# Gated attention layer on one core: the channel mix drawn into the attention's program

## The reference

```python
    x = x + jnp.tanh(g_xattn[0]) * _L0_xattn_ref(_layernorm(x, axis=-1), ctx_1024, ctx_1024, mask_BxS2_if1, ...)
    x = x + jnp.tanh(g_ffn[0]) * _L0_ffn_ref(_layernorm(x, axis=-1), L0_ffn_W_r, L0_ffn_W_k, L0_ffn_W_v, L0_ffn_mu_r, L0_ffn_mu_k)
```

```python
            x_prev = jnp.concatenate([jnp.zeros((B, 1, C), x.dtype), x[:, :-1, :]], axis=1)
            xr = mu_r * x + (1.0 - mu_r) * x_prev
            xk = mu_k * x + (1.0 - mu_k) * x_prev
            r = jax.nn.sigmoid(jnp.einsum('btc,dc->btd', xr, W_r))
            k = jnp.einsum('btc,dc->btd', xk, W_k)
            k_act = jnp.square(jax.nn.relu(k))
            out = r * jnp.einsum('btc,dc->btd', k_act, W_v)
```

## Time and profile before

| | us |
|---|---|
| median of 3 runs | 2034.28 (2032.4 to 2034.94) |
| the profiled execution's own time | 2038.13 |
| its span, first to last instruction | 2036.4 |
| PE busy | 1932.5 (95%) |
| DVE busy | 1379.0 (68%) |
| POOL busy | 1295.2 (64%) |
| ACT busy | 971.1 (48%) |

### The profile page before, as it was taken

How to read it: one execution, slowest core, us unless ns; L and a number is a source line. 1 busy time by engine, 2 the same in 40 slices (tenths; PEclk the granted TensorE clock), 3 DMA queues, 4 the chain that set the end, 5 groups by cost and what they waited for, 6 DMA issues and landing times. The chain is left out here.

```text
span 2036.4 us, 36616 instructions
## 1 busy us (share of the span) xinstructions
PE 1932.5 (95%) x11648; PEld 1501.0 (74%) x11648; DVE 1379.0 (68%) x3534; ACT 971.1 (48%) x1870; POOL 1295.2 (64%) x1829
## 2 busy tenths in 40 slices
PE   5899999999999999999999999995599999999999
PEld 3677777777777777777777777772488888888887
DVE  3777777776777767777677777764466575656663
ACT  3555555555555555555555555544243433334341
POOL 4566666666666666666666666656277787777771
PEclk8999999999999999999999999996799999999999
DMA  5545555455554455545555445552122323132211
GB/s 182 108 114 123 128 144 124 113 123 126 144 123 114 122 128 144 118 119 121 129 144 118 118 123 127 126 145 64 62 83 82 103 72 113 67 106 74 98 67 62
DMA packets 128665, 229.31 MB, mean 113 GB/s; under 512 B 18656, under 2 KB 20704, under 8 KB 127616
## 3 DMA queue, kind: packets, MB, share of 16 engines
q1 hardware_dynamic: 128512, 227.43, 42.2%
HBM read 92.06 MB, written 33.59 MB: 62 GB/s over the span
## 5 line engine op out<-in xcount | busy, mean ns | idle before, releaser
L701 DVE CUSTOM_DVE_ANT_0 score_ps<-score_ps,causal 128x128 f32<-128x128 f32 (+3 forms) x1024 | 487.1, 504 | 295.1 <-PE score_ps L855 294.0
L533 ACT ACTIVATE probs<-prob_ps 128x512 f32<-128x512 f32 (+1 forms) x768 | 395.7, 527 | 412.3 <-PE prob_ps L879 209.2
L855 PE MATMUL score_ps<-k_stack,q_stack 97*128 97x128 f32 (+3 forms) x1024 | 319.5, 353 | 6.6 <-DVE least L701 2.9
L879 PE MATMUL prob_ps<-q_stack,k_stack 100*128 100x512 f32 (+3 forms) x1024 | 285.6, 320 | 20.4 <-DMA q_stack<-max_rows 14.3
L385 POOL TENSOR_SCALAR_AFFINE_SELECT probs<-probs 128x256 f32<-128x256 f32 x256 | 106.5, 416 | 271.7 <-ACT probs L533 271.7
L396 POOL TENSOR_TENSOR prob_sum<-probs 128x384 f32<-128x384 f32 x256 | 263.9, 1031 | 0.0
L855 PEld LDWEIGHTS score_ps<-k_stack,q_stack 97*128 97x128 f32 x1024 | 189.4, 191 | 53.5 <-issue 13.3
L879 PEld LDWEIGHTS prob_ps<-q_stack,k_stack 100*128 100x128 f32 x1024 | 193.6, 192 | 42.8 <-DMA q_stack<-max_rows 19.1
L399 POOL TENSOR_TENSOR prob_sum<-prob_sum,probs 128x256 f32<-128x256 f32 x256 | 188.8, 738 | 36.7
L389 POOL TENSOR_SCALAR_AFFINE_SELECT probs<-probs 128x256 f32<-128x256 f32 x256 | 105.0, 410 | 157.0 <-ACT probs L533 156.8
L896 PE MATMUL value_ps<-probs,v 128*32 128x512 f32 (+3 forms) x2048 | 154.8, 443 | 13.2 <-POOL prob_sum L399 13.2
(11 more groups left out here) (145 smaller groups left out, 4918.0 us busy)
## 6 DMA issues: line engine op xcount, KB each, us to landing
k_stack<-staged_k_high SPq DMA_DIRECT2D x256, 128.0 KB
q_stack<-staged_q_high SPq DMA_DIRECT2D x256, 128.0 KB, 3.1
tiles<-in_x SPq DMA_DIRECT2D x16, 1024.0 KB, 5.7
k_stack<-staged_k_low SPq DMA_DIRECT2D x128, 128.0 KB
q_stack<-staged_q_low SPq DMA_DIRECT2D x128, 128.0 KB, 3.2
x_io<-in_x SPq DMA_DIRECT2D x16, 1024.0 KB, 7.2
x<-x_io SPq DMA_DIRECT2D x64, 256.0 KB, 3.3
wk_low_room<-x SPq DMA_DIRECT2D x16, 1024.0 KB, 5.5
```

The lines of the kernel that those rows point to most:

```text
L533: nc.scalar.activation(probs[:, u % RING, lo:hi], prob_ps[(3 * u + c) % 2][:, 0:hi - lo], ACT.Exp, scale=SCALE).then_inc(exp_done, 1)
L701: nc.vector.tensor_tensor_reduce(out=here, in0=here, in1=causal[:, LATE - P * t:S], scale=-1.0, scalar=3e38, op0=ALU.add, op1=ALU.min, acc ...
L855: last = nc.tensor.matmul(here[:, at:at + P * (t + 1)], q_stack[n][0:MASK_ROW + 1, j, P * t:P * t + P], k_stack[n][0:MASK_ROW + 1, j, 0:P ...
L879: last = nc.tensor.matmul(here[:, at:at + width], k_stack[n][0:ROWS, j, P * k:P * k + P], q_stack[n][0:ROWS, j, P * k:S], start=True, stop ...
```

## The change

The two blocks become one function, `gated_layer`. Rooms are shared inside it: the mixed parts lie where Wq and Wk lay, squares where q and k were staged, gates, result and Wv in the stacks. The hardware loop is written out.

1. The tables. `WORK` is as before. A second table holds PE's pieces for slots N-4 to N+2, where fk and fr are the k and r projections of the channel mix of batch 0. The transposes of x1 of batch 0 stand in slots N-6 and N-5.

```diff
+        LAST_WORK = {
+            N - 4: ("", "", ""),
+            N - 3: ("", "fk0 0", "fk0 12"),
+            N - 2: ("fk0 3", "fk1 01", "fk1 23"),
+            N - 1: ("fk2 01", "fk2 23", "fk3 01"),
+            N: ("", "fk3 23", "fr0 01"),
+            N + 1: ("fr0 23", "fr1 01", "fr1 23"),
+            N + 2: ("fr2 0", "fr2 12", "fr2 3"),
+        }
```

```diff
+            def scale_earlier(e):
...
+                wait(act, mixed_done, e - 1)
+                col = "kr".index(n)
+                nc.scalar.activation(earlier[:, e % 2, 1:S], ffn_xT[:, k, 0:S - 1], ACT.Identity, scale=mu_rest[:, col, k:k + 1]
+                                     ).then_inc(scaled, 1)
...
+            def mix_tokens(e):
+                j, n, k = mix_tile(e)
+                dve.wait_ge(scaled, e + 1)
+                dve.wait_ge(mu_loaded, 16 * 2)
+                wait(dve, mix_low, e - 1)
```

3. The layernorm of the channel mix is applied by ACT instead of POOL. The relu goes straight into `square`, which DVE squares in place:

```diff
+                nc.scalar.activation(square[:, g, :], k_ps[g % 2][:], ACT.Relu).then_inc(relu_done, 1)
...
+                nc.vector.tensor_tensor(square[:, g, :], square[:, g, :], square[:, g, :], ALU.mult).then_inc(square_done, 1)
```

5. ACT's mixing work in the last slots (the tiles of batch 0 on DVE stand beside it in the same slots):

```diff
+                if i == N - 4:
+                    split_ffn("r")
+                    high_part_mix(1)
+                    scale_earlier(2)
+                if i == N - 3:
+                    scale_earlier(4)
+                    high_part_mix(3)
```

6. ACT in a round j of the rest, after its relus and casts:

```diff
-                gate_r(i, 0)
-                if has_next:
-                    high_part_mix(i + 1, "k", 0, k_done)
-                    high_part_mix(i + 1, "k", 1, k_done)
-                gate_r(i, 1)
...
+                for m in range(T):
+                    gate_r(j, m)
+                if j + 1 < B:
+                    mix_steps(j + 1, "k")
+                    mix_steps(j + 1, "r")
+                if j + 2 < B:
+                    for m in range(T):
+                        apply_layernorm(B + j + 2, m)
```

7. PE after the slots: the last r block, the last `values`, transposes of batch 1, the output projection of batch 15, and then the v projection of batch 0 and the rounds 1 to 15:

```diff
+            for k in range(K):
+                project_fr(0, 3, k)
+            values(N // HG - 1)
+            transpose_x(B + 1, 0)
+            transpose_x(B + 1, 1)
...
+            def project_fv(j, m, k):
...
+                elif k == 0:
+                    pe.wait_ge(y_done, T * j + m - 1)
```

More of the change, by code:

```diff
@@ L563, in first, with gate_r @@
+            def gate_r(j, m):
+                act.wait_ge(fr_done, T * j + m + 1)
+                act.wait_ge(y_done, T * (j - 1) + m + 1)
+                nc.scalar.activation(r_tanh[:, m, :], r_ps[m % 2][:], ACT.Tanh, scale=0.5).then_inc(r_ready, 1)
             def first(i, b, s):
@@ L612, in fourth @@
                     high_part_c(b + 1, 2 * (s - 11) + 1)
-                if has_next and b >= 0 and s in (6, 7):
+                if now and s in (6, 7):
                     apply_layernorm(b + 1, 2 * (s - 6) + 1)
@@ L780, in third @@
                     normalise((i - VALUES) // HG)
-                if has_next and b >= 0 and s == 3:
+                if now and s == 3:
                     layernorm_stats(b + 1, 0)
+                if i == N - 4:
+                    mix_tokens(1)
+                    low_part_mix(0)
+                if i == N - 3:
+                    low_part_mix(2)
+                if i == N - 2:
+                    mix_tokens(4)
+                    low_part_mix(4)
+                if i == N - 1:
+                    square_k(0, 1)
+                if i == N:
+                    for m in range(T):
+                        layernorm_stats(B + 1, m)
                 if has_next and s == 10:
@@ L840, in _, with mix_k, mix_r_and_combine @@
                 slot(i)
+            def mix_k(j):
+                e = 2 * K * j
+                mix_tokens(e)
+                for k in range(1, K):
+                    mix_tokens(e + k)
+                    low_part_mix(e + k - 1)
+                low_part_mix(e + K - 1)
+            def mix_r_and_combine(j):
+                e = 2 * K * (j + 1) + K
+                mix_tokens(e)
+                for k in range(1, K):
+                    mix_tokens(e + k)
+                    low_part_mix(e + k - 1)
+                    combine(j, k - 1)
+                low_part_mix(e + K - 1)
+                combine(j, K - 1)
+            correct(N // HG - 1)
+            refine(N // HG - 1)
+            normalise(N // HG - 1)
+            low_part_attn(N // HG - 1)
+            for m in range(T):
+                add_output(B - 1, m)
+            mix_k(1)
+            for m in range(T):
+                layernorm_stats(B + 2, m)
+            aggregate_stats(B + 2)
+            mix_r_and_combine(0)
+            for j in range(1, B):
+                for g in range(K):
+                    square_k(j, g)
+                if j + 2 < B:
+                    for m in range(T):
+                        layernorm_stats(B + j + 2, m)
+                    aggregate_stats(B + j + 2)
+                if j + 1 < B:
+                    mix_k(j + 1)
+                    mix_r_and_combine(j)
+                else:
+                    for m in range(T):
+                        combine(j, m)
         @block.tensor
@@ new lines, in project_fr @@
+            def project_fr(j, m, k):
+                if m == 0:
+                    pe.wait_ge(mix_low, 2 * K * j + K + k + 1)
+                    pe.wait_ge(ffn_low["r"], 1)
+                if k == 0 and j == 0 and m < 2:
+                    pe.wait_ge(scores_read, T * N)
+                elif k == 0 and j == 0:
+                    pe.wait_ge(r_copied, m - 1)
+                elif k == 0:
+                    pe.wait_ge(r_ready, T * j + m - 1)
+                last = exact_product(nc, r_ps[m % 2][:], lambda k: [part[:, k, P * m:P * m + P] for part in mix["r"]],
+                                     lambda k: [part[:, k, :] for part in ffn_w["r"]], [k], k == 0, k == K - 1)
+                if k == K - 1:
+                    last.then_inc(fr_done, 1)
@@ L1122, in iteration @@
+            for m in range(T):
+                for k in range(K):
+                    project_fv(0, m, k)
+            for j in range(1, B):
+                for g in range(K):
+                    for k in range(K):
+                        project_fk(j, g, k)
+                    if j + 1 < B and g < T // 2:
+                        transpose_x(B + j + 1, 2 * g)
+                        transpose_x(B + j + 1, 2 * g + 1)
                 for m in range(T):
-                    load_res(i, m)
```

790 lines of the change are left out of this document (390 added, 400 removed).

## The result

The changed kernel takes 2074.05 us (median of 4 runs, 2073.26 to 2075.65) against 2034.22 us (4 runs, 2032.4 to 2034.94): a ratio of 1.0198, with a 95% interval of 1.0183 to 1.0213. It is slower by 39.8 us; the forecast was 56 slower, 2090 us, with a range of 2050 to 2115.

The account below looks back on a forecast made before the run. PE was taken as the bound, busy 95% of the span, with a hole at the handover. Handover -39, small things +4 and rounds +91 us gave +56 on 2034.3: 2090 us, range 2050 to 2115.

Parts of the forecast that it names:

- The handover: From slot N-4 to round 1 of the channel mix: 95 us against 134, a gain of 39.
- The slots: Slots N-4 to N-1 of the handover, set by DVE and ACT: 36 us, a gain of 14.
- slot N to round 1: Second stretch of the handover: 59 us against 112, of which 6 for stretches at half clock.
- The wait of a round: Third v block in rounds 1 to 14: PE waits 4.5 us for DVE's first combination, `y`, behind ACT's scalings.
- The clock: Behind each round's wait PE runs at half clock: 2.0 us lost a round, bounds 0 and 3.4.
- A round as a whole: Rounds 1 to 14 of the channel mix: 4.5 us of wait plus 2.0 of clock, 91 us in all.
- PE's work is the same: Channel mix rounds: PE's own work stays unchanged, with matmul starts 0.233 us apart and 35.34 us a round.
- The signs named ahead: Signs in the changed profile, among them rounds of 41 to 43 us and a last one of 33 to 35.
- Small things: Weight splits, one more batch's layernorm and transposes in earlier slots, small DMAs at the start: a loss of 4 us.
- The clock holds: Rival: a single wait in dense work does not lower the clock; a round loses 4.5 us, 2062 us; chance 0.13.
- The release comes in time: Rival: `y` comes by 5.6 us after the v start, rounds stay at 35.3 us; 1999 us, chance 0.09.
- The last slots are worse: Rival: DVE and ACT wait tile by tile, handover gains only 29, 7.9 us lost a round; 2121 us, chance 0.06.

Follow-up runs that it names:

- shifted versions: The kernel before with 48 or 496 unused bytes a partition behind the transposed x of the channel mix: 2036.12 us and 2035.33 us.

## Why the prediction was right, and where not

**The handover: right, for partly other reasons.** 95 us were forecast and 95.6 measured, a gain of 38.4 instead of 39. The slots took 34.0 instead of 36, slot N to round 1 took 61.5 instead of 59. The wait at batch 0's third v block was forecast at 6.9 and is 6.41. Inside, errors cancel, and that the sum is right to 0.6 us is luck: I had reckoned with no wait at the last `values`, where POOL's small steps cost 5.06 us, and with no hold of DVE under POOL's 4.94 us. From slot N on the rows show what made up for half of the first: PE was busy for 50.1 us where the sum had 51.6 with its half clock, and the waits beside the o projection and at the third v block were 1.0 us shorter than forecast. In the slots other steps were priced too high, where I laid ACT's and DVE's steps end to end; which ones, no run here shows. The wait for the maxima's DMA fell from 6.32 us to 1.10.

**The wait of a round: right.** 4.5 us forecast, 4.43 measured, in each of rounds 1 to 14, put down to `y`. The new scaling takes 0.71 to 0.75 us in the rows (0.72 assumed). By the 58 cycles of the Trainium skill ("VectorE: DVE Perf Modes", section "The TRN2 errata") the wait was an estimate of 3.4 us; the trace decides for the rows, with 4.43. The two runs that moved only ACT's order or only DVE's show the mechanism from both sides.

**The clock: right in size, not as a rule.** 2.0 us a round were forecast; 40.94 - 34.46 - 4.43 = 2.05. But the step "after an idle 2.8 us PE ran 3.4 us at half clock" can't be carried to shorter waits as a rule: two of three of 2.37 us cost none, and one of 1.66 us did.

**A round as a whole: 6.5 forecast, 5.60 measured.** Against its own execution the sum was 21 us too high (56 forecast, 35.1 in the spans): 14 x 0.9 = 12.6 in these rounds, 1.0 in the last, and 7.7 in the small things below. The step that failed is "PE's work is the same", where I priced it by matmul starts 0.233 us apart. They are 0.227 apart in the changed rounds: 34.46 us for a round where the sum had 35.34. The signs named ahead missed by the same pace: a round of 40.94 us where 41 to 43 stood, and a last one of 32.8 us for PE where 33 to 35 stood. Against the changed kernel's own pace the loss is 6.48, as forecast. The trace of before couldn't show this: its rounds have the one pace only.

**Small things: wrong in sign.** 4 us of loss were forecast before slot N-4, and it begins 3.7 us earlier. The starts of `values` place it: the last slots do lose, 2.4 us from slot N-16 to N-4 (2 to 3 forecast). But the program's start is 3.6 us faster by the first `values` (76.89 against 80.44 us). In 11 profiles with the changed start it comes at 74.8 to 77.8 us, in three of the kernel before and its shifted versions at 78.1 to 80.4: the stretch from 26 to 40 us has the full clock in all 11 and 0.88 to 0.91 in the three. Why, no run here shows. The other 2.5 us of the attention are less than the 3.8 us by which the profiles with the changed attention differ among themselves there.

**The rivals.** "The clock holds" is out for waits of 4.43 us. "The release comes in time" named the right lever: with it in time the kernel is faster, 1982.8 us, where 1999 was worked out for it; of the 16 us between them 13 are the pace again. "The last slots are worse" did not come.

## What to carry to other kernels

Before an instruction is put behind another on an in-order engine, ask who waits for what stands behind it: here 8 us of free DVE time in front of a chain of 11 steps cost PE 6.5 us a round, and a few moved lines on ACT gave 91 us back. When the largest wait of a round is taken away, look for the next one at once (it was 1.69 us here, again one line away), and don't judge a large restructuring by its first order: the same program was 2% slower and 2.5% faster. A long POOL instruction is not free because POOL is: here each of two held a DVE operation on two SBUF inputs until it had ended.

## What was not expected of the hardware

- A matmul of 512 columns starts 0.227 or 0.233 us after the one before at the same granted clock, by where its operand lies: 16 or 64 bytes more ahead of `kact` slowed the v blocks from 2.72 to 2.80 us, and them alone. Which property of the address decides isn't known.
- Half clock behind a wait comes whole or not at all. Waits of 4.43 us always brought it; of 2.37, one in three; of 1.84, 7 of 13; of 1.69, none of 13; of 1.60 and 0.99, none of six; but the one of 1.66, at another place, did.
- DVE was held for 4.22 and 4.52 us by one POOL instruction of 4.94 and 4.54. The other way round, sixteen small steps of POOL took 4.5 us beside an idle DVE and 7.5 to 8.4 beside a busy one.
